# Small VectorE steps placed singly between the products and scans of a selective-state kernel

## The chip, the cores and the metric

One core of one Trainium2 chip runs the whole program. The metric is the device time of one execution in microseconds (us), inputs in HBM to outputs in HBM. Engines are named as in the profile: PE is TensorE, DVE is VectorE, ACT is ScalarE, POOL is GpSimd, SP is SyncE, which here only issues DMAs.

## What is computed

One block over eight batch elements of 512 tokens by 128 channels, all float32. `silu(c) @ wmod` gives scale, shift and gate for each element. Then comes a Mamba-like layer with 256 inner channels, kept as two halves of 128 (`Q = 2`), and 16 states for each channel (`NS = 16`). Then a mixture of experts with a shared expert.

```python
h = layernorm(x) * (1 + ca) + sa
xz = h @ in_proj_w.T                      # x part: causal conv of 4 taps, silu -> u; z part: gate
dt, B, C = split(u @ x_proj_w.T)
delta = softplus(dt @ dt_w.T + dt_b)
state = state * exp(delta * A) + (delta * u) * B      # scan over 512 tokens, per channel and state
y = (sum_n state * C + u * D) * silu(z)
x = x + ga * (y @ out_proj_w.T)
h = layernorm(x) * (1 + cb) + sb
p = softmax(h @ router_w + router_b)      # the two largest of 8 are kept, ties by index
x = x + gb * (shared_expert(h) + sum_e p_e * expert_e(h))   # gelu experts, 128 -> 256 -> 128
```

## The kernel before

**Stages.** The work on the eight elements is pipelined by hand. `pipeline` calls each engine's `slots(b, a, n, m)` eight times: in one slot element `b` is scanned, `a = b - 1` goes through its output projection, second norm, router, experts and residual, `n = b + 1` through convolution, projections and softplus, and `m = b + 2` is loaded and normalised. A slot is called a period here. Each engine runs its instructions strictly in the order in which its own `slots` lists them; only semaphores tie the engines to each other. So the order of the lines is the schedule.

**The scan.** An element has 16 units of 2 states by 512 tokens. For each, ACT makes the decays (`decays`, L885), DVE the product `bc * du` into one PSUM tile (`scan_input`, L1197) and the scan itself (`scan`, L1206), POOL multiplies the state with C (`readout`, L433), and PE adds that into the two Y banks with 8 transposing matmuls (`y_add`, L516). Product `u+1` waits for scan `u` because they share the PSUM tile; scan `u` waits for `yacc_done` of unit `u-4` (a ring of four states); POOL's product `u` waits for DVE's product `u+1` too ("paced"). I call the place after a product and before its scan a P-S gap, and the place after a scan and before the next product an S-P gap. There are 16 of each in a period.

**Element `a` in the same slot.** When unit 15 of `a` is added (`y_add(a, 15)`), DVE multiplies with the gate (`gate_y`, L1216). Then `g_transpose`, `out_proj`, `att_transpose` on PE with `g_rows` and `att_rows` on ACT; `residual` (L1226) with the statistics of the second norm (L1230, L1235) on DVE; `make_rstd` (L420, L423) on POOL; `x1hat` (L1244) on DVE; `x1_transpose` (L616) on PE; `h2_rows` (L992, L995) on ACT; `router` on PE; `split_h2` (L1310) and `logits` (L1254 to L1260) on DVE; `router_e`, a table load and 18 `gelu` (L1014) on ACT beside 18 `up` blocks of three matmuls on PE (L645 to L647), which share three banks; `top2` (L1268 to L1294) on DVE makes the weights `w9`; `weights_transpose` (L654) and `weights_out` (L1007) turn them; then `shared_down` (L662), eight `down` blocks and eight `mix_scaled` / `mix_add`, `acc_rows` (L987), `acc_transpose` (L696) and on DVE `finish` (L1315). Between these PE carries the `y_add`s of `b`. `keep_busy` (L611) issues transposes whose result nobody reads.

**Elements `n` and `m`.** `make_delta` on DVE (L1170 to L1179) ends softplus in four steps after ACT's exponential and logarithm (L957); `delta_x` (L1186) makes `delta * u`. ACT's `skip_term(n)` (L916) and the decays of `n` wait for `delta_done`. `stats` and `xhat` (L1147 to L1158) normalise `m`.

Of the kernel before, what the change touches and what calls it, by code (L numbers as in the profile page):

```python
# [60 lines left out]
def adaln_mamba_moe_kernel(nc, x, in_proj_w, conv_w, conv_b, x_proj_w, dt_w, dt_b, a_log, d_skip,  # L61
# [5 lines left out]
    with ExitStack() as ctx:  # L67
# [25 lines left out]
        before = sb("before", [P, E, E], mybir.dt.bfloat16)  # L93
# [21 lines left out]
        bn = sb("bn", [P, NT, 6])  # L115
        mean_var = sb("mean_var", [P, 2, NT, 2])
# [188 lines left out]
        def _(sp):  # L305
# [47 lines left out]

            def slots(b, a, n, m):
                first_batch = n and isinstance(n.i, int) and n.i == 0
                if m and first_batch:
                    sp.wait_ge(xT_done, m.i)
                    load_x(m)
                if n:
# [3 lines left out]
                if m and n and not first_batch:  # L363

                    load_x(m)
# [3 lines left out]
                if n:  # L369
                    load_bc(n, 0)  # L370
# [3 lines left out]
                if a:  # L374
                    sp.wait_ge(out_done, a.i + 1)
                    sp.dma_start(out[a.i].rearrange("(t p) d -> p t d", p=P),
                                 out_sb[:, :, :]).then_inc(out_stored, 16)
                if b and not is_last(b):

                    load_residual(b)  # L380
                if n:
                    load_bc(n, 1)
                if b and b.i == 1:
# [7 lines left out]
            def tail(a):  # L391
                for t in range(NT):
# [9 lines left out]
        def _(pool):  # L402
            pool.memset(ident[:, :], 0.0).then_inc(const_made, 1)
            pool.memset(before[:, :, :], 1.0).then_inc(const_made, 1)
# [9 lines left out]
            pool.affine_select(out=before[:, :, :], in_=before[:, :, :], pattern=[[1, E], [-1, E]],  # L414
                               compare_op=ALU.is_gt, fill=0.0, base=0,
# [40 lines left out]
        def _(pe):  # L456
# [243 lines left out]
            def slots(b, a, n, m):  # L700
# [44 lines left out]
                if a:  # L745
                    keep_busy(a, n, 5 if b else 12)
# [710 lines left out]
```

## Time and profile before

| | |
|---|---|
| median of 3 runs | 685.6 us (685.33 to 688.16) |
| the profiled execution | 684.8 us, its span 683.1 us |
| DVE busy | 598.3 us, 88% of the span, 713 instructions |
| PE busy | 593.3 us, 87%; weight loads 466.5 us |
| ACT, POOL busy | 489.7 us, 72%; 320.2 us, 47% |
| DVE scans L1206 | 292.2 us in 128, 2283 ns each |
| DVE products L1197 | 157.6 us in 128, 1231 ns each |
| POOL products L433 | 300.1 us in 127, 2363 ns each |
| PE read-out sums L516 | 139.0 us in 1024 matmuls |
| mean DMA rate | 114 GB/s |

Busy shares of two engines near 90% say only that both are candidates. What one waits for, and in which stage, is in the waits and in the timeline. PE's busy time counts pipelined matmuls with a modelled end, so the distance between the starts of two groups is the better measure of what PE needs.

### The profile page before, as it was taken

What the parts mean: (1) busy time and instruction counts of PE and PEld (TensorE: products, weight loads), DVE (VectorE), ACT (ScalarE), POOL (GpSimd) and SP (SyncE); (2) the same over time, 40 slices, a digit from 0 to 9 for tenths busy, and PEclk for the clock granted to TensorE, in tenths of its full rate; (3) what the DMA queues carried; (4) which work ended last, traced back from release to release, by engine and by line L of the source; (5) the groups of instructions that cost most, each with busy time, mean ns of one, the idle gap of its engine ahead of it and who ended that gap; (6) DMA issues with size and microseconds to landing.
All of it is one profiled execution on the core that took longest, in us unless ns stands there. A gap on an engine that the chain in (4) does not pass through costs nothing.

```text
span 683.1 us, 9767 instructions
## 1 busy us (share of the span) xinstructions
PE 593.3 (87%) x3646; PEld 466.5 (68%) x3646; DVE 598.3 (88%) x713; ACT 489.7 (72%) x861; POOL 320.2 (47%) x171
## 2 busy tenths in 40 slices
PE   5684478899989998999989998999979947998897
PEld 4243345689657965788567966787668936798686
DVE  5399999999999999999999999999998999798416
ACT  3689535999589976989589957998598925962460
POOL 1036556446654556446653656446543664464000
PEclk9787589999999999999999999999999968999999
DMA  7423333314432235133531343223522442220000
GB/s 221 161 92 140 123 139 142 125 70 169 163 128 82 108 128 184 62 124 124 173 124 63 124 160 138 83 103 124 179 103 70 176 156 83 103 78 16 1 1 16
DMA packets 26705, 77.87 MB, mean 114 GB/s; under 512 B 3025, under 2 KB 17570, under 8 KB 18466
## 3 DMA queue, kind: packets, MB, share of 16 engines
q1 hardware_dynamic: 26178, 76.82, 31.1%
q8 instruction: 29, 0.48, 0.3%
q10 hardware_dynamic: 480, 0.43, 0.2%
q14 instruction: 18, 0.15, 0.1%
HBM read 74.61 MB, written 2.62 MB: 113 GB/s over the span
## 4 chain that ended last, share of the span: by engine, by line
PE 53%; DVE 31%; issue 7%; ACT 5%; POOL 2%; DMA 1%; DVEq 0%; POOLq 0%; ACTq 0%
DVE state L1206 15%; PE psum L677 12%; PE psum L516 10%; DVE psum L1197 8%; PE psum L543 5%; PE psum L645 5%; PE psum L647 4%; PE psum L646 4%; PE psum L687 3%; POOL state L433 2%; PE psum L662 2%; PE psum L565 1%; ACT L866 1%; DVE out_sb L1244 1%; PE psum L799 1%
## 5 line engine op out<-in xcount | busy, mean ns | idle before, releaser
L433 POOL TENSOR_TENSOR state<-state,bc 128x1024 f32<-128x1024 f32 x127 | 300.1, 2363 | 291.8 <-DVE psum L1197 291.8
L1206 DVE TENSOR_TENSOR_SCAN state<-decay,psum 128x1024 f32<-128x1024 f32 x128 | 292.2, 2283 | 21.9 <-PE psum L516 9.5
L885 ACT ACTIVATE decay<-delta,a_neg 128x511 f32<-128x511 f32 x256 | 166.1, 729 | 10.4 <-DVE state L1206 10.3
L516 PE MATMUL psum<-ident,state 128*128 128x128 f32 x1024 | 139.0, 283 | 33.6 <-POOL state L433 33.4
L1197 DVE TENSOR_TENSOR psum<-bc,du 128x1024 f32<-128x1024 f32 x128 | 157.6, 1231 | 4.8 <-DVE state L1206 0.5
L516 PEld LDWEIGHTS psum<-ident,state 128*128 128x128 f32 x1024 | 120.3, 146 | 56.0 <-POOL state L433 44.9
L677 PE MATMUL psum<-down_w,h 128*128 128x128 f32 x896 | 109.9, 276 | 0.0
L677 PEld LDWEIGHTS psum<-down_w,h 128*128 128x128 f32 x896 | 104.4, 192 | 5.3 <-issue 5.3
L1014 ACT ACTIVATE h<-psum,vec 128x512 f32<-128x512 f32 x144 | 97.0, 688 | 2.1 <-PE psum L647 0.6
L980 ACT ACTIVATE gT_mix<-psum,w 128x128 f32<-128x128 f32 x224 | 64.8, 388 | 20.0 <-PE psum L687 14.4
L645 PE MATMUL psum<-h_hi,up_hi 128*128 128x512 f32 x144 | 59.2, 411 | 10.7 <-DVE h_lo L1310 6.7
L543 PE MATMUL psum<-h_sb,conv_in_wT 128*128 128x512 f32 x128 | 59.9, 614 | 8.8 <-ACT h_sb L895 8.8
L647 PE MATMUL psum<-h_hi,up_lo 128*128 128x512 f32 x144 | 57.7, 401 | 0.0
L646 PE MATMUL psum<-h_lo,up_hi 128*128 128x512 f32 x144 | 57.6, 400 | 0.0
L543 PEld LDWEIGHTS psum<-h_sb,conv_in_wT 128*128 128x128 f32 x128 | 24.3, 199 | 34.6 <-issue 25.4
L645 PEld LDWEIGHTS psum<-h_hi,up_hi 128*128 128x128 f32 x144 | 27.5, 191 | 20.5 <-DVE h_lo L1310 7.3
L687 PE MATMUL psum<-ident,gT_mix 128*128 128x128 f32 x224 | 33.9, 274 | 0.0
L647 PEld LDWEIGHTS psum<-h_hi,up_lo 128*128 128x128 f32 x144 | 27.4, 190 | 6.7
L646 PEld LDWEIGHTS psum<-h_lo,up_hi 128*128 128x128 f32 x144 | 27.6, 191 | 6.0
L687 PEld LDWEIGHTS psum<-ident,gT_mix 128*128 128x128 f32 x224 | 26.0, 141 | 1.5 <-ACT gT_mix L980 1.5
L611 PE MATMUL psum<-ident 128*128 128x128 f32 x210 | 26.2, 273 | 0.0
L906 ACT ACTIVATE du<-psum,vec 128x512 f32<-128x512 f32 x16 | 10.8, 687 | 21.2 <-PE psum L543 18.7
(151 smaller groups left out, 638.3 us busy)
## 6 DMA issues: line engine op xcount, KB each, us to landing
bc<-bc_rows SPq DMA_DIRECT2D x64, 1024.0 KB, 4.7
x_sb<-_attn_hidden_states_dram SPq DMA_DIRECT2D x9, 256.0 KB, 2.8
x<-_attn_hidden_states_dram SPq DMA_DIRECT2D x7, 256.0 KB, 3.0
out_dram<-out_sb SPq DMA_DIRECT2D x7, 256.0 KB, 2.4
h<-in_L_ffn_rw_dram SPq DMA_DIRECT2D x1, 1024.0 KB
bc_rows<-rows SPq DMA_DIRECT2D x8, 64.0 KB, 4.8
h<-in_L_wmod_dram ACTq DMA_DIRECT2D x1, 384.0 KB
h<-in_L_attn_in_proj_w_dram SPq DMA_DIRECT2D x1, 256.0 KB, 4.7
```

The source lines that it names most:

```text
L433: pool.tensor_tensor(state[:, u % STATE_RING, :, :], state[:, u % STATE_RING, :, :], bc[:, pair % BC_RING, 1, first:first + NU, :], ALU.mu ...
L516: last = nc.tensor.matmul(Y[q][:, t * P:(t + 1) * P], state[:, u % STATE_RING, s, t * P:(t + 1) * P], ident[:, :], start=False, stop=(u in ...
L543: last = nc.tensor.matmul(A[q], conv_in_wT[:, q, k, :], h_sb[:, k:k + L], start=(k == 0), stop=(k == KC - 1))
L645: nc.tensor.matmul(bank, high, h2_hi[:, :], start=True, stop=False)
L646: nc.tensor.matmul(bank, high, h2_lo[:, :], start=False, stop=False)
L647: nc.tensor.matmul(bank, low, h2_hi[:, :], start=False, stop=True).then_inc(up_done, 1)
L677: last = nc.tensor.matmul(A[j % 2][:, e * DM:(e + 1) * DM], h1[:, (group * EG + e) * HQ + q, ts], down_w[:, group * EG + e, q, :], start=( ...
L687: last = nc.tensor.matmul(OUTP[:, t * P:(t + 1) * P], mix[:, j % 2, e, :], ident[:, :], start=False, stop=(j == DOWNS - 1 and e == EG - 1) ...
L885: last = nc.scalar.activation(decay[:, r, s, 1:L], delta[:, b.p, q, 1:L], ACT.Exp, scale=a_neg[:, q, k:k + 1])
L1014: nc.scalar.activation(h1[:, m, :], UP_RING[m % 3], ACT.Gelu, bias=vec[:, bias:bias + 1]).then_inc(gelu_done, 1)
L1197: nc.vector.tensor_tensor(IN, bc[:, pair % BC_RING, 0, first:first + NU, :], du[:, b.p, q:q + 1, :].broadcast_to([P, NU, L]), ALU.mult).th ...
L1206: nc.vector.tensor_tensor_scan(state[:, u % STATE_RING, :, :].rearrange("p n t -> p (n t)"), decay[:, u % DECAY_RING, :, :].rearrange("p n ...
```

## The change

- **DVE.** `stats`, `xhat`, `make_delta` and `top2` are cut into single steps. `scan_slots` writes out all gaps of a period by hand and puts one or a few steps into each of 15 P-S gaps and 8 S-P gaps, where before 4 and 6 held any. `residual` and the statistics of the second norm (`stats2`) move from the P-S gap of unit 3 to the S-P gap after scan 2, `x1hat` from after scan 3 to the P-S gap of unit 3, `split_h2` to after scan 3, `logits` to the P-S gap of unit 4. `finish(a - 1)` moves from the end of a period into the next one.
- **Ties.** A table of `1 - 2^-24` and 1 (`tie_scale`) replaces the mask `before`; the comparison needs a scaling and one comparison instead of two comparisons, a product and a sum: two DVE steps fewer for each element.
- **Element `m`.** Its statistics are taken one period earlier (`late`), into a tile of their own (`bn_in`), aggregated in the P-S gap of unit 0, and `xhat` follows in four places up to unit 5.
- **POOL.** `make_rstd` for `m` comes right after product 15 of `a`. `make_rstd` for `a` comes ahead of product 2, and product 2 also waits for `x1hat` to be done.
- **PE.** The three `y_add`s 2, 3 and 4 come after `up` 2, 8 and 14, instead of ahead of the router, after all `up`s, and after `weights_transpose`. `keep_busy` has 24 and 10 transposes instead of 14 and 5. `x_transpose` comes ahead of `down` 2.
- **SP.** The output of `a - 1` is stored at the head of the next slot, then the residual of `a` is loaded; the load of `x` waits for `x_transpose` and lies behind pair 3 of B and C.

```diff
@@ SP slots
-                if m and n and not first_batch:
-                    load_x(m)
+                if a and a.i > 0:
+                    store(Batch(a.i - 1, 1 - a.p))
+                if a:
+                    load_residual(a)
...
+                if b and m and m.i + 1 < B:
+                    sp.wait_ge(xT_done, m.i + 1)
+                    load_x(Batch(m.i + 1, 1 - m.p))
@@ POOL slots
+                if m and (a or not b):
+                    make_rstd(0, stats_done, rstd_eps, rstd_done, m)
                 for u in range(UN - 1):
+                    if a and u == 2:
+                        make_rstd(1, stats2_done, rstd2_eps, rstd2_done, a)
+                        pool.wait_ge(xhat2_done, a.i + 1)
                     if b:
                         readout(b, u)
-                    if a and u == 2:
-                        make_rstd(1, stats2_done, rstd2_eps, rstd2_done, a)
-                    if m and u == 5:
+                    if m and b and not a and u == 1:
                         make_rstd(0, stats_done, rstd_eps, rstd_done, m)
@@ PE slots
-                    keep_busy(a, n, 14)
+                    keep_busy(a, n, 24)
                     x1_transpose(a)
-                if b:
-                    y_add(b, 2)
-                if a:
-                    keep_busy(a, n, 5 if b else 12)
+                    keep_busy(a, n, 10)
                     router(a)
-                    for k in range(M_UP):
+                for k in range(M_UP):
+                    if a:
                         up(a, n, k)
-                if b:
-                    y_add(b, 3)
+                    if b and k in (2, 8, 14):
+                        y_add(b, 2 + (k - 2) // 6)
                 if a:
                     weights_transpose(a)
-                if b:
-                    y_add(b, 4)
                 if a:
                     shared_down(a)
@@ DVE, top2
-                nc.vector.tensor_tensor(gt_eq[:, 1, :, :, :], other, mine, ALU.is_equal
-                nc.vector.tensor_tensor(gt_eq[:, 0, :, :, :], other, mine, ALU.is_gt
...
+                nc.vector.tensor_tensor(
+                    gt_eq[:, 1, :, :, :], pr[:, :, :].unsqueeze(3).broadcast_to([P, NT, E, E]),
+                    tie_scale[:, :, :].unsqueeze(1).broadcast_to([P, NT, E, E]),
+                    ALU.mult).then_inc(prob_step, 1)
...
+                nc.vector.tensor_tensor(
+                    gt_eq[:, 0, :, :, :], pr[:, :, :].unsqueeze(2).broadcast_to([P, NT, E, E]),
+                    gt_eq[:, 1, :, :, :], ALU.is_gt).then_inc(prob_step, 1)
```

The new order of DVE in a period, with I for `scan_input` and S for `scan`: I0 aggr_x, S0 finish(a-1), I1 gate_y, S1 xhat 0 and 1, I2 xhat 2, S2 residual and stats2, I3 x1hat, S3 split_h2, I4 logits, S4, I5 xhat 3, S5 prob_sum, relu_plus_exp and prob_inverse, I6 probs, S6 tie_bars and beaten, I7 ranks, S7 weights, I8, S8 rounded_exp, I9 minus_rounded, S9, I10 plus_log 0, S10, I11 plus_log 1, S11, I12 bn_x 0, S12, I13 bn_x 1, S13, I14 delta_x, S14, I15 bn_x 2 and 3, S15.

## Rows read from the trace of the kernel before

**Rows 1.** The page, chain that ended last: share of the span by engine.

```profile
PE 53%; DVE 31%; issue 7%; ACT 5%; POOL 2%; DMA 1%; DVEq 0%; POOLq 0%; ACTq 0%
```

**Rows 2.** Stretches: length; busy us of PE, PEld, DVE, ACT, POOL; PE's clock; DMA.

```profile
34.00:110.00 76.00, 47.71 (x195) 30.19 (x196) 72.65 (x60) 48.93 (x73) 38.78 (x19) 0.75 0.34 128
334.96:409.97 75.01, 70.70 (x448) 55.67 (x447) 71.49 (x82) 61.65 (x111) 40.15 (x20) 1.00 0.35 125
```

**Rows 3.** DVE timeline, period 4: start us, length us, line, out<-in, idle before.

```profile
333.81 1.23 DVE L1197 TENSOR_TENSOR psum<-bc,du 128x1024 f32<-128x1024 f32 x1
334.96 1.22 DVE L1216 TENSOR_TENSOR gT_mix<-psum,z_silu 128x1024 f32<-128x1024 f32 x1
336.11 2.28 DVE L1206 TENSOR_TENSOR_SCAN state<-decay,psum 128x1024 f32<-128x1024 f32 x1
338.42 1.23 DVE L1197 TENSOR_TENSOR psum<-bc,du 128x1024 f32<-128x1024 f32 x1
339.78 2.29 DVE L1206 TENSOR_TENSOR_SCAN state<-decay,psum 128x1024 f32<-128x1024 f32 x1
...
343.25 0.69 DVE L1226 TENSOR_TENSOR x<-psum,x 128x512 f32<-128x512 f32 x1
...
345.18 2.25 DVE L1206 TENSOR_TENSOR_SCAN state<-decay,psum 128x1024 f32<-128x1024 f32 x1
347.35 1.09 DVE L1244 TENSOR_SCALAR out_sb<-x,mean_var,rstd 128x128 f32<-128x128 f32 x4
```

**Rows 4.** PE timeline, period 4.

```profile
333.83 1.09 PE L516 MATMUL psum<-ident,state 128*128 128x128 f32 x8
...
345.05 1.69 PE L611 MATMUL psum<-ident 128*128 128x128 f32 x14
348.49 0.66 PE L616 MATMUL psum<-ident,out_sb 128*128 128x128 f32 x4 [1.75 <-DVE out_sb L1244]
...
355.54 0.50 PE L645 MATMUL psum<-h_hi,up_hi 128*128 128x512 f32 x1 [0.53 <-ACT h L1014]
...
368.40 1.96 PE L662 MATMUL psum<-h,down_w 128*128 128x512 f32 x4
...
373.22 1.04 PE L516 MATMUL psum<-ident,state 128*128 128x128 f32 x8
```

**Rows 5.** POOL timeline, just ahead of period 4's `gate_y`: product 15 of `a`.

```profile
331.44 2.34 POOL L433 TENSOR_TENSOR state<-state,bc 128x1024 f32<-128x1024 f32 x1 [1.80 <-DVE psum L1197]
```

**Rows 6.** DVE timeline, the same period, `delta_x` in an S-P gap.

```profile
390.11 2.29 DVE L1206 TENSOR_TENSOR_SCAN state<-decay,psum 128x1024 f32<-128x1024 f32 x1
392.31 1.20 DVE L1186 TENSOR_TENSOR du<-du,delta 128x1024 f32<-128x1024 f32 x1
393.43 1.23 DVE L1197 TENSOR_TENSOR psum<-bc,du 128x1024 f32<-128x1024 f32 x1
```

**Rows 7.** DVE by line and shape: busy us, mean ns; one removed step.

```profile
L1283 DVE TENSOR_TENSOR gT_mix<-gT_mix,before 128x256 f32<-128x256 f32 x8 | 3.4, 425 | 0.3
```

**Rows 8.** DVE timeline, end phase: `x1hat` with no scan ahead of it.

```profile
640.07 1.11 DVE L1244 TENSOR_SCALAR out_sb<-x_sb,mean_var,rstd 128x128 f32<-128x128 f32 x4 [1.40 <-POOL rstd L423]
```

**Rows 9.** ACT timeline, period 4.

```profile
350.53 2.55 ACT L885 ACTIVATE decay<-delta,a_neg 128x511 f32<-128x511 f32 x4
...
367.67 0.58 ACT L1007 ACTIVATE rows<-psum 9x512 f32<-9x512 f32 x1 [0.62 <-PE psum L654]
...
381.48 1.34 ACT L916 ACTIVATE skip<-du,vec 128x512 f32<-128x512 f32 x2
...
394.29 1.14 ACT L980 ACTIVATE gT_mix<-psum,w 128x128 f32<-128x128 f32 x4 [0.57 <-PE psum L687]
```

**Rows 10.** DVE timeline, period 6: `gate_y`, scan 7 with its wait, scan 9.

```profile
484.99 1.23 DVE L1216 TENSOR_TENSOR gT_mix<-psum,z_silu 128x1024 f32<-128x1024 f32 x1
...
517.52 2.29 DVE L1206 TENSOR_TENSOR_SCAN state<-decay,psum 128x1024 f32<-128x1024 f32 x1 [2.85 <-PE psum L516]
...
529.20 2.29 DVE L1206 TENSOR_TENSOR_SCAN state<-decay,psum 128x1024 f32<-128x1024 f32 x1
```

More of the change, by code:

```diff
@@ L1319, in slots @@
                 if b:
-                    scan_input(b, 0)
-                    scan(b, 0)
-                    scan_input(b, 1)
+                    scan_slots(b, a, n, m)
+                    return
+                if m:
+                    for t in range(NT):
+                        bn_x(m, t)
+                    nc.vector.memset(pace, 0.0)
+                    aggr_x(m)
+                    for t in range(NT):
+                        xhat(m, t)
+                if n:
+                    split_up_weights()
+                    relu_plus_exp(n)
+                    rounded_exp(n)
+                    minus_rounded(n)
+                    for q in range(Q):
+                        plus_log(n, q)
+                    delta_x(n)
@@ new lines, in scan_slots @@
+            def scan_slots(b, a, n, m):
+                late = Batch(m.i + 1, 1 - m.p) if m and m.i + 1 < B else None
+                new = m if b.i == 0 else None
+                old = m if b.i > 0 else None
+                scan_input(b, 0)
+                if new:
+                    bn_x(new, 0)
+                    bn_x(new, 1)
+                if old:
+                    aggr_x(old)
+                scan(b, 0)
+                if a and a.i > 0:
+                    finish(Batch(a.i - 1, 1 - a.p))
+                scan_input(b, 1)
+                if new:
+                    bn_x(new, 2)
+                    bn_x(new, 3)
@@ L1363, in slots @@
-                for u in range(8, UN):
-                    if b:
-                        scan_input(b, u)
-                    if a:
-                        if u == UN - 1:
-                            finish(a)
-                    if b:
-                        scan(b, u)
-                    if n and u == 12:
-                        delta_x(n)
+                scan(b, 4)
+                if new:
+                    xhat(new, 0)
+                    xhat(new, 1)
+                    xhat(new, 2)
@@ new lines, in scan_slots @@
+                scan_input(b, 11)
+                if n:
+                    plus_log(n, 1)
+                scan(b, 11)
+                scan_input(b, 12)
+                if late:
+                    bn_x(late, 0)
+                scan(b, 12)
+                scan_input(b, 13)
+                if late:
+                    bn_x(late, 1)
+                scan(b, 13)
+                scan_input(b, 14)
+                if n:
+                    delta_x(n)
+                scan(b, 14)
+                scan_input(b, 15)
@@ L1374, in last_readout @@
+                if late:
+                    bn_x(late, 2)
+                    bn_x(late, 3)
+                scan(b, 15)
             def last_readout(b):
```

204 lines of the change are left out of this document (118 added, 86 removed).

## The prediction

> **What bounds the kernel now.** The page shows DVE and PE busy for nearly the same share, so I read the chain of work that ended last first: PE holds 53% of it and DVE 31% [rows 1]. Neither engine sets the pace alone. The stretches say why: in a middle period of 75.01 us DVE is busy for 71.49 and PE for 70.70, at full clock [rows 2]. There are 8 periods. Period 0 has no element `a`: PE is busy for 47.71 of 76 us there, at a mean clock of 0.75, and DVE for 72.65 [rows 2]. Period 0 is DVE's, the middle ones belong to a loop through both.
>
> I measure that loop from the start of `gate_y`, called G; in one middle period G is 334.96 [rows 3] and the next G 409.97 [rows 2]. DVE works on from G almost without idle time. PE's loop is: gate, transposes and projection, `x1hat`, router, `up`, `down`, convolution, y_add 15, gate. POOL's product 15 ends at 331.44 + 2.34 = 333.78 and y_add 15 starts at 333.83 [rows 4, 5]: PE waited for it. The matmuls ahead of it would have let it start some 0.3 us earlier (an estimate: a y_add that waited takes 1.09, and the ones in a stream start 0.87 apart). So PE's own loop is about 74.7 us, DVE's 75.0. This is what to see: PE is 0.3 us behind being the bound.
>
> **DVE: what the gaps are worth.** A plain unit is product at 338.42, scan at 339.78: 1.36 apart, and from a scan to the next product 2.31 (336.11 to 338.42). With `gate_y` (1.22) in a P-S gap the scan comes 2.30 after the product, so the step costs 0.94 of its 1.22 [rows 3]: the gap holds some 0.3 us in which DVE only waits for its own product. `delta_x` (1.20) in an S-P gap makes 3.32 from scan to product instead of 2.31, so it costs 1.0 [rows 6]: 0.2 saved. Eleven more P-S gaps and two more S-P gaps are filled: 11 x 0.3 + 2 x 0.2 = 3.7 us, less where a step is shorter than the gap (bn_aggr, xhat 2 and 3, bn_x and probs nearly vanish, but save no more than they took). `finish` and the second norm change from P-S to S-P and lose 0.1 each. Two tie steps of 0.425 go [rows 7]: 0.9 with their dependence. I add up gap by gap and get 71.0 us for DVE's period, 4.0 less.
>
> The Trainium skill, page "VectorE: DVE Perf Modes", section "The DRAIN you can't avoid", says that a next op waits until the pipe is empty and that semaphores between chained ops cost nothing, which would leave only the removed steps, some 0.9 us. The rows above differ with it, since a step put into a P-S gap is partly free, and I go by the rows.
>
> **PE's loop, with each new term.** All times are from G.
>
> *To x1hat.* The chain gate to `att_transpose` is unchanged; its product, `residual`, starts at 8.29 now [rows 3], but is ready earlier: I put the end of `att_transpose` at 7.3 (an estimate: y_adds 0 and 1, some 1.8 us, end at 10.1 [rows 4], and one `dt_proj` of about 0.9 lies between). In the new order scan 1 is at 1.15, xhat 0 and 1 at 3.36, product 2 at 3.87, xhat 2 at 5.02, scan 2 at 5.27 and `residual` at 7.48, so it doesn't wait. With its statistics it takes 1.93 (343.25 to 345.18). Product 3 is at 9.41. `x1hat` comes 1.40 after the last statistic where nothing covers POOL's work [rows 8]: 10.9. It ends at 12.0, against 13.48 now (347.35 + 1.09).
>
> *A cost that no row shows.* POOL's add and power, most of the 1.40 [rows 8], will run beside product 3, which reads two SBUF tensors; in the old order they lie beside a scan. No row shows the two together. Cost from 0 to 1.07, the rest of product 3 that POOL would have to wait for (below 0 is excluded: POOL was idle anyway). It reaches PE with at most 0.46, because PE itself arrives late: y_add 0 and 1 end at 10.09 (345.05), 24 fillers take 24/13 of what 13 pitches of the 14 took, 2.6 us [rows 4], so `x1_transpose` can start only at 12.7. I take the middle, 0.23.
>
> The Trainium skill, page "SBUF — State Buffer", section "Who interferes with whom", says that a GpSimd instruction and a VectorE one with two SBUF inputs exclude each other for the whole instruction. By it the upper end holds. No row bears it out or speaks against it.
>
> *Router and up.* `x1_transpose` is at 12.7 instead of 13.53, so `split_h2`, ready at 14.9, makes DVE wait 0.75. `up` 3 waits for the first gelu, and that for `router_e` behind four decays (2.55 [rows 9]): 355.54 is 20.58 now [rows 4], then 19.8. y_add 2 lies in that wait, free, as it was ahead of the router. Gain 0.8.
>
> *To shared_down.* From `up` 3 to `shared_down` PE takes 12.86 (355.54 to 368.40) with y_adds 3 and 4 and `weights_transpose` in it. The same matmuls now end in `up` 17 at 32.1. `weights_transpose` waits for w9, which DVE reaches after scan 7, at 32.6: 0.5 lost. Then `weights_out` (0.58 [rows 9]) and its hand-overs have no cover, since y_add 4 has moved: 0.8 lost. `shared_down` starts at 33.95 (34.2 with the 0.23), now at 33.44. Loss 0.5 to 0.75.
>
> *Softplus.* delta is finished by plus_log 1 in the gap of unit 11. Scan 9 has to wait for y_add 5, which starts 4.8 after `shared_down` and takes 1.04 [rows 4]: 39.9. Two units and two such steps further delta is done, at 48.1. ACT reaches `skip_term` at 46.52 now (381.48 [rows 9]) and at about 47.1 then: it waits 1.0, which with its later start makes it 1.1 to 1.3 further behind PE. Its slack against PE is the 0.57 ahead of the last mix step [rows 9]. So 0.4 to 0.7 of PE's loop; I take 0.5. If that slack were not there, it would be 1.1.
>
> *x_transpose, fillers, SP, POOL.* `x_transpose` is the same work earlier. The 5 extra fillers after it lie in the wait for ACT's h2. If that wait were gone they would cost 0.5. On SP the store and the residual load are queued ahead of the rows of `n`, and the load of x behind pair 3 of B and C; `finish` runs well before G, so x1 has over 7 us to land, and B and C of pair 2 are requested only after product 3, so they lose nothing. If a load were late, `residual` or bn_x would wait for it, and DVE has 4 us of slack. On POOL product 2 and all behind it wait for `x1hat`. It starts at 12.1; y_add 2 wants it at 18, so nobody waits.
>
> PE's loop: 74.7 + 0.75 + 0.5 = 75.9, against 75.0 now. DVE's 71.0 is idle time at `gate_y`. Periods 1 to 5: 5 x 0.9 = **+4.5**.
>
> **The other periods.** Period 0 is DVE's. It has no steps of `a`; of those left, seven longer ones or pairs lie in P-S gaps against one before: 6 x 0.3 = 1.8, and xhat 3 and the four bn_aggr nearly vanish, 0.4: -2.2. POOL's `make_rstd` comes beside product 1 of the next period, and product 3 of this one; by the same unknown 0 to 1.2, taken as 0.6: **-1.6**. In period 6 scan 7 waits 2.85 for y_add 3 behind all `up`s [rows 10], and nothing of PE is late afterwards, as there is no convolution behind it. That wait goes; what is late next is y_add 5 at scan 9. Scan 9 is 44.21 after that period's G (529.20 - 484.99) [rows 10] and will be at 40.1; the rest is DVE's and 0.4 dearer: **-3.7**. In period 7, where PE has no work of `n` either, I let the same wait move to scan 9 nearly whole: **-0.3**, an estimate between 0 and -0.7. The end phase holds the same chain; two tie steps less lie beside `up`: 0.
>
> Sum: 684.8 - 1.6 + 4.5 - 3.7 - 0.3 = 683.7 for the profiled execution. The median of the runs is 0.8 above it: **684.5**.
>
> **Rivals.**
> - *DVE keeps the pace.* If the hand-overs (w9, weights_out, skip_term) are covered and the transposes gain more than 0.8, PE's loop falls below 75. At the end DVE's 71.0 decides: 5 x -4 - 6 = 658. Half way, a loop of 73.5: 685.6 - 7.5 - 6 = 672. For it: each loss is under 1 us and three must all be there. Against: PE's work from `shared_down` on (40 us to y_add 15) is the same and none of it waits for DVE.
> - *ACT and PE lose more* (slower). From the point at which ACT is more than 0.57 behind, each further us late in delta reaches every middle period whole. Steps of DVE with two SBUF inputs (minus_rounded, plus_log, delta_x) now start beside POOL's products; if each costs 0.4, and the 1.07 is whole, the loop is 77.3: 5 x 2.3 - 4 = +7.5, 693.
> - *POOL first.* If POOL's product got going ahead of the step in the gap, and they exclude each other, each of six steps would wait about 2.3 us: 14 us a period, less 5 of slack, over 730. Against: a step starts 1.15 after the product's start (334.96 - 333.81) [rows 3], before the product's 1.23 are over, and POOL's product is released only by that end.
> - *The gaps are no cheaper.* The change then doesn't do what it says: DVE's period is 74.1, the loop stays PE's, period 0 gives 0.5 and period 6 3: 686.5.
>
> **Chances.** Forecast 0.50 (its own range 680 to 689), DVE keeps the pace 0.23, ACT and PE lose more 0.19, POOL first 0.03, gaps no cheaper 0.05. The range, 672 to 694, leaves out the far halves of the outer cases. A measurement of this kernel tells about 0.5% (3.4 us) from no change. Faster by more: most of the second case and a quarter of the first, 0.34; slower by more: 0.22; within: 0.44.
>
> **What would show it.** Right: DVE's idle time goes from some 1 us in a middle period to 4 or 5, nearly all at `gate_y` waiting for y_add 15; G to G 75.5 to 76.3; y_add 15 no longer waits for POOL; `weights_transpose` waits for w9 and `shared_down` for `weights_out`; ACT waits for delta at `skip_term`; scan 7 of period 6 doesn't wait, scan 9 does; products of POOL up to 2.36 + 1.2 long where a two-input step shares the gap, if they exclude each other, and `rstd` 1 us later. Wrong: G to G under 74.7, with DVE without idle time; or DVE steps in P-S gaps with starts far above 1.15 after their product.

## The result, and the profile after

The kernel before took 685.47 us (median of 4 runs), the changed one 706.14 us (704.89 to 709.51): a ratio of 1.030, 95% interval 1.027 to 1.034. It is slower by 20.7 us, where the prediction had 684.5 in a range of 672 to 694. The profiled execution took 709.51 us with a span of 707.7, the slowest of the four.

From the starts of `gate_y` (G) in each trace come the lengths of the periods, the measure by which all kernels of this document are compared. P2 is the period that begins with the second G; "to G1" is what lies ahead of the first.

| us | to G1 | P1 | P2 | P3 | P4 | P5 | P6 | P7 |
|---|---|---|---|---|---|---|---|---|
| before | 109.7 | 75.03 | 75.03 | 75.19 | 75.01 | 75.02 | 75.90 | 68.74 |
| changed | 110.2 | 78.14 | 81.73 | 78.17 | 79.12 | 78.17 | 73.98 | 73.34 |

P1, P3 and P5 are 3.0 to 3.2 us longer, and P2 (6.7), P4 (4.1) and P7 (4.6) lose more. P6 gains 1.9. The first view is that of stretches: length, busy us of PE, PEld, DVE, ACT and POOL, PE's granted clock. It answers to [rows 2].

```profile
348.19:427.31 79.12, 73.77 (x463) 58.12 (x462) 71.32 (x77) 61.56 (x111) 43.65 (x20) 0.98 0.34 118
505.48:579.46 73.98, 64.78 (x438) 53.63 (x436) 69.89 (x65) 57.58 (x105) 40.24 (x18) 0.99 0.29 105
```

DVE is busy for 71.32 us of P4 in spite of two tie steps less, against 71.49 before. Something on DVE became longer. The chain of work that ended last has moved too, to ACT above all ([rows 1] had 5%):

```profile
PE 38%; DVE 33%; ACT 12%; issue 8%; DMA 5%; POOL 3%; SPq 0%; DVEq 0%; POOLq 0%; ACTq 0%
```

The waits name the hand-over (engine, line, what it waited for: total us, times, the longest):

```profile
DVE gT_mix L1228 <- PE psum L525: 21.4, 7, 4.0
...
ACT gT_mix L1006 <- DVE gT_mix L1275: 16.1, 8, 2.0
PE psum L654 <- ACT h L1019: 16.0, 6, 2.7
```

Line 1275 is the third step of `logits`. DVE's timeline in P4 (G = 348.19), and under it POOL's, show it:

```profile
360.93 2.28 DVE L1218 TENSOR_TENSOR_SCAN state<-decay,psum 128x1024 f32<-128x1024 f32 x1
363.24 0.76 DVE L1329 TENSOR_TENSOR h_lo<-h,h_hi 128x512 fp32r<-128x512 f32 x1
363.92 1.22 DVE L1209 TENSOR_TENSOR psum<-bc,du 128x1024 f32<-128x1024 f32 x1
365.06 0.18 DVE L1269 TENSOR_TENSOR gT_mix<-psum,router_bias 128x32 f32<-128x32 f32 x1
365.27 0.19 DVE L1273 TENSOR_REDUCE router_stats<-gT_mix 128x4 f32<-128x32 f32 x1
365.49 2.17 DVE L1275 TENSOR_TENSOR gT_mix<-gT_mix,router_stats 128x32 f32<-128x32 f32 x1
367.58 2.27 DVE L1218 TENSOR_TENSOR_SCAN state<-decay,psum 128x1024 f32<-128x1024 f32 x1
```

```profile
357.69 1.09 POOL L426 TENSOR_TENSOR rstd<-mean_var,constants 128x4 f32<-128x4 f32 x1 [2.00 <-DVE mean_var L1250]
358.85 1.01 POOL L429 TENSOR_TENSOR rstd<-rstd,constants 128x4 f32<-128x4 f32 x1
361.09 2.37 POOL L439 TENSOR_TENSOR state<-state,bc 128x1024 f32<-128x1024 f32 x1 [1.23 <-DVE out_sb L1259]
365.22 2.39 POOL L439 TENSOR_TENSOR state<-state,bc 128x1024 f32<-128x1024 f32 x1 [1.77 <-DVE psum L1209]
```

A step on 128x32 elements takes 2.17 us: it ends at 367.66, right behind POOL's product 3 (365.22 + 2.39 = 367.61). The step of the same size ahead of it, a reduction, takes 0.19 with that product beside it. In the changed kernel all seven `logits` that lie beside a product of POOL have such a third step (2.02 to 2.17), and the eighth, in the end phase with POOL idle, takes 0.19. In the kernel before, where `logits` stood behind a scan, it took 0.19 every time. Likewise POOL's add ahead of `rstd` takes 1.09 beside product 3 of DVE, and 0.20 elsewhere.

What that does to PE, in PE's timeline of P4, to be laid beside [rows 4]:

```profile
370.07 0.79 PE L654 MATMUL psum<-h_hi,up_hi 128*128 128x512 f32 x1 [2.68 <-ACT h L1019]
370.66 0.63 PE L655 MATMUL psum<-h_lo,up_hi 128*128 128x512 f32 x1
371.08 0.63 PE L656 MATMUL psum<-h_hi,up_lo 128*128 128x512 f32 x1
...
383.71 0.60 PE L663 MATMUL psum<-ident,w 128*9 128x128 f32 x4
385.35 1.95 PE L671 MATMUL psum<-h,down_w 128*128 128x512 f32 x4 [1.04 <-ACT rows L1012]
```

`up` 3 starts at G + 21.88, after PE stood for 2.68 us; before it was G + 20.58 with 0.53. In this period the first matmuls behind the wait start 0.43 us apart instead of 0.235, until 372.79: the granted clock is 0.50 in that stretch, the lower of its two levels (1.2 of 2.4 GHz). `shared_down` starts at G + 37.16 here and at G + 36.2 in the periods without that, against 33.44.

P2 has a cause of its own, on SP's queue (start us, issue time) and then on DVE:

```profile
182.72 0.43 SPq L389 DMA_DIRECT2D gate_row<-gateT  x1
192.92 0.32 SPq L391 DMA_DIRECT2D gate_row_sb<-gate_row  x1
193.29 0.43 SPq L357 DMA_DIRECT2D out_dram<-out_sb  x1
193.76 0.51 SPq L352 DMA_DIRECT2D x<-_attn_hidden_states_dram  x1
```

```profile
199.27 0.69 DVE L1238 TENSOR_TENSOR x<-psum,x 128x512 f32<-128x512 f32 x1 [3.49 <-DMA x<-_attn_hidden_states_dram]
```

`gate_row`'s round trip through DRAM, done once, holds SP for 10.2 us (182.72 to 192.92). The store and the residual's load now stand behind it, so `residual` waits 3.49 us.

### The profile page after: what moved, and what is told of

It is laid out like the page before. It is cut to its first block, busy times and chain, and to the rows that moved or that the text cites. A ratio compares the mean times of both kernels' runs of the same rounds, so it can differ in the third digit from the quotient of the medians.

```text
span 707.7 us, 9968 instructions
## 1 busy us (share of the span) xinstructions
PE 616.1 (87%) x3751; PEld 483.4 (68%) x3751; DVE 597.2 (84%) x691; ACT 488.1 (69%) x861; POOL 346.5 (49%) x171
## 4 chain that ended last, share of the span: by engine, by line
PE 38%; DVE 33%; ACT 12%; issue 8%; DMA 5%; POOL 3%; SPq 0%; DVEq 0%; POOLq 0%; ACTq 0%
DVE state L1218 17%; DVE psum L1209 9%; PE psum L525 6%; PE psum L552 5%; ACT gT_mix L985 3%; ACT decay L890 3%; PE psum L686 3%; PE psum L620 2%; POOL state L439 2%; PE psum L602 2%; PE psum L671 2%; PE psum L654 2%; PE psum L655 2%; PE psum L656 2%; DMA x_sb<-_attn_hidden_states_dram 2%
## 5 line engine op out<-in xcount | busy, mean ns | idle before, releaser
L439 POOL TENSOR_TENSOR state<-state,bc 128x1024 f32<-128x1024 f32 x127 | 318.2, 2505 | 270.1 <-DVE psum L1209 261.5
L654 PE MATMUL psum<-h_hi,up_hi 128*128 128x512 f32 x144 | 62.7, 435 | 17.4 <-ACT h L1019 16.0
L552 PE MATMUL psum<-h_sb,conv_in_wT 128*128 128x512 f32 x128 | 61.8, 630 | 9.2 <-ACT h_sb L900 9.2
L655 PE MATMUL psum<-h_lo,up_hi 128*128 128x512 f32 x144 | 59.9, 416 | 0.0
L656 PE MATMUL psum<-h_hi,up_lo 128*128 128x512 f32 x144 | 59.4, 412 | 0.0
L654 PEld LDWEIGHTS psum<-h_hi,up_hi 128*128 128x128 f32 x144 | 29.0, 201 | 25.1 <-ACT h L1019 17.8
L620 PE MATMUL psum<-ident 128*128 128x128 f32 x315 | 38.3, 275 | 0.0
L620 PEld LDWEIGHTS psum<-ident 128*128 128x128 f32 x315 | 35.5, 142 | 0.5 <-issue 0.5
L426 POOL TENSOR_TENSOR rstd<-mean_var,constants 128x4 f32<-128x4 f32 x16 | 9.4, 588 | 44.6 <-DVE mean_var L1250 31.3
```

The costliest lines, as they stand in the source:

```text
L439: pool.tensor_tensor(state[:, u % STATE_RING, :, :], state[:, u % STATE_RING, :, :], bc[:, pair % BC_RING, 1, first:first + NU, :], ALU.mu ...
L552: last = nc.tensor.matmul(A[q], conv_in_wT[:, q, k, :], h_sb[:, k:k + L], start=(k == 0), stop=(k == KC - 1))
L620: nc.tensor.transpose(A[1][:, 0:P], ident[:, :], ident[:, :])
L654: nc.tensor.matmul(bank, high, h2_hi[:, :], start=True, stop=False)
L655: nc.tensor.matmul(bank, high, h2_lo[:, :], start=False, stop=False)
L656: nc.tensor.matmul(bank, low, h2_hi[:, :], start=False, stop=True).then_inc(up_done, 1)
```

## The experiments

Each kernel was timed beside the one before on the same chip; the ratio is to that. The first table gives the periods of all of them, and the texts behind it what each is. They are told in the order of the argument; e1 to e4 ran first, then c1, e5, e6 and e8, then d1, c1f and c2, and d2 to d4 last.

| kernel | median us | ratio (95%) | P1 | P2 | P3 | P4 | P5 | P6 | P7 |
|---|---|---|---|---|---|---|---|---|---|
| e1 | 692.08 | 1.007 (1.003 to 1.010) | 76.55 | 79.07 | 76.29 | 76.26 | 77.63 | 71.77 | 69.11 |
| e2 | 704.26 | 1.025 (1.020 to 1.031) | 78.15 | 78.16 | 79.17 | 78.15 | 78.18 | 75.15 | 70.17 |
| e3 | 707.94 | 1.030 (1.024 to 1.036) | 78.15 | 80.66 | 79.48 | 78.18 | 79.74 | 74.46 | 72.16 |
| e4 | 721.25 | 1.050 (1.045 to 1.055) | 80.78 | 79.68 | 80.96 | 79.66 | 80.66 | 80.51 | 72.29 |
| e6 | 696.62 | 1.017 (1.011 to 1.023) | 78.07 | 76.14 | 77.96 | 78.05 | 76.16 | 77.02 | 69.43 |
| e8 | 710.07 | 1.036 (1.031 to 1.041) | 79.31 | 79.26 | 78.34 | 78.17 | 79.24 | 79.04 | 71.49 |
| e5 | 726.30 | 1.057 (1.051 to 1.064) | 81.14 | 84.35 | 81.80 | 81.35 | 80.12 | 77.17 | 74.50 |
| d1 | 691.77 | 1.008 (1.005 to 1.010) | 76.68 | 79.33 | 76.40 | 76.38 | 77.76 | 72.05 | 67.82 |
| d2 | 688.03 | 1.002 (0.998 to 1.006) | 74.54 | 82.47 | 74.57 | 74.56 | 74.57 | 72.69 | 68.41 |
| d3 | 682.78 | 0.995 (0.992 to 0.997) | 74.54 | 74.58 | 74.58 | 74.58 | 75.96 | 72.66 | 68.51 |
| d4 | 703.41 | 1.024 (1.019 to 1.029) | 78.06 | 76.55 | 77.91 | 78.07 | 78.07 | 74.58 | 72.29 |
| c1 | 680.55 | 0.990 (0.987 to 0.994) | 75.39 | 75.37 | 75.36 | 75.33 | 75.32 | 72.15 | 66.99 |
| c1f | 681.34 | 0.992 (0.988 to 0.995) | 75.36 | 75.03 | 75.02 | 75.02 | 75.02 | 72.13 | 67.72 |
| c2 | 675.98 | 0.984 (0.980 to 0.988) | 73.88 | 74.74 | 74.74 | 73.88 | 73.91 | 72.71 | 68.00 |

### Is it POOL's product that holds the step?

**e1**, in the changed kernel's POOL slots:

```
 if b and a and u == 3:
     pool.wait_ge(lg_step, 3 * a.i + 3)      # added: product 3 waits for logits
 if b:
     readout(b, u)
```

> The changed kernel with one wait more: POOL's product 3 waits until the three steps of logits are done. Theory A (exclusion): the third step of logits, with two SBUF inputs, was held for 2.17 us by POOL's product 3. Here it takes 0.19, up 3 starts some 2 us earlier (G + 19.9 instead of G + 21.9), POOL's product starts about 1 us later and nobody waits for it; middle periods of 76.2 instead of 78.2 us, and with period 7 the whole is 14 to 18 us shorter, 688 to 692 us. Theory B (the hand-overs of w9 and weights_out, the fillers and the late delta carry the loss): the third step is beside the path, and the time changes by less than 3 us, 703 to 708.

DVE's and PE's timelines in P4 (G = 343.17):

```profile
360.25 0.19 DVE L1275 TENSOR_REDUCE router_stats<-gT_mix 128x4 f32<-128x32 f32 x1
360.47 0.19 DVE L1277 TENSOR_TENSOR gT_mix<-gT_mix,router_stats 128x32 f32<-128x32 f32 x1
```

```profile
363.07 0.50 PE L656 MATMUL psum<-h_hi,up_hi 128*128 128x512 f32 x1 [0.71 <-ACT h L1021]
363.41 0.39 PE L657 MATMUL psum<-h_lo,up_hi 128*128 128x512 f32 x1
```

The step takes 0.19, `up` 3 starts at G + 19.90, the `up`s run at full clock, P4 is 76.26 and the median, 692.1, is at the upper end of what was expected: Theory A. One added wait on POOL, an engine with time to spare, gives back 14 of the 20.7 us. P2 and P5 of e1 stay longer, P2 by the wait for a load that is shown above, and P5 by 1.4 us because `y_add` 0 and 1 ran slowly, as in d3 below.

**e4** makes the one step from the other side, in the kernel before:

```
-                    logits(a)                # behind split_h2, ahead of product 5
 scan_input(b, 5)
+if a: logits(a)
 scan(b, 5)
```

> The kernel before with one part of the change alone: logits moved from behind split_h2 (ahead of product 5) to behind product 5 (ahead of scan 5). Theory A (exclusion): POOL's product 4 is released by the end of product 5 and holds the third step of logits for about 2.1 us instead of 0.19; logits ends 3.5 us later, up 3 starts some 3.5 us later, of which PE's loop has 0.3 to spare: periods 3.0 to 3.6 longer, times 6 or 7, 18 to 25 us: 704 to 710. Theory B (no exclusion, a step in a product-scan gap is partly free): the third step takes 0.19, logits ends 1.5 us later, periods 1.2 longer: +7 to +8.5 us, 693 to 694, with DVE 0.3 us a period better off.

**e6** is e4 with POOL's product 4 waiting for `logits`:

> The same as e4 (the kernel before with logits in the gap of product 5), but POOL's product 4 waits for logits. Theory A (exclusion): the third step takes 0.19, logits ends 1.15 later than before the change, up 3 at G + 21.7 instead of 23.7, periods of 75.9 to 76.5 instead of 79.7 to 80.7; 692 to 697 against 721 for e4. Theory B (the place in the gap itself, or DVE's waits, made e4 slow): no less than 710.

e4's third step takes 2.20 us and `up` 3 starts at G + 23.71; with POOL held back (e6) it takes 0.19 and `up` 3 starts at G + 21.7. 721 against 697 us: with all that follows from each, the place in the gap costs some 10 us by itself and POOL's product 25 more. e6's median lies in Theory A's 692 to 697, but only P2 and P5 are in its 75.9 to 76.5. In P1, P3 and P4 (78.0) the matmuls from `up` 3 to `up` 17 take 11.6 to 11.9 us instead of 9.93, although PE's wait ahead of them is no longer there than in P2 (0.5 to 1.0 us; P2's is 1.67). In P4 (G = 344.09) the lower clock sets in at the end of `up` 1, in a row of matmuls without a gap and some 1.5 us ahead of that wait:

```profile
363.03 0.50 PE L649 MATMUL psum<-h_hi,up_lo 128*128 128x512 f32 x1
363.33 0.63 PE L647 MATMUL psum<-h_hi,up_hi 128*128 128x512 f32 x1
363.76 0.63 PE L648 MATMUL psum<-h_lo,up_hi 128*128 128x512 f32 x1
```

So the wait ahead of `up` 3 isn't the only thing that takes the clock down. e4 itself was over its expected 704 to 710, and its periods grew by 4.65 to 5.8 us where `up` 3 is only 3.1 later. PE's timeline of e4's P4 shows where the rest is:

```profile
374.68 0.79 PE L645 MATMUL psum<-h_hi,up_hi 128*128 128x512 f32 x1 [3.67 <-ACT h L1014]
375.27 0.63 PE L646 MATMUL psum<-h_lo,up_hi 128*128 128x512 f32 x1
375.70 0.63 PE L647 MATMUL psum<-h_hi,up_lo 128*128 128x512 f32 x1
```

### What a wait of PE costs besides itself

**e8** is e4 with filler transposes in PE's wait:

```
 for k in range(M_UP):
+    if k == 3:
+        pe.wait_ge(lg_step, 3 * a.i + 1)
+        for _ in range(32):
+            nc.tensor.transpose(MISC[:, 0:P], ident[:, :], ident[:, :])
     up(a, n, k)
```

> The same as e4, with 32 filler transposes (0.11 us each) on PE between up 2 and up 3, where PE is idle for 3.67 us and the following up matmuls start 0.43 instead of 0.235 apart. Theory A (the idle time lets the clock fall, and that adds to the wait): up 3 starts at G + 23.7 as in e4, all matmuls behind it are 0.235 apart, from up 3 to up 17 it takes 9.95 instead of 11.5 to 12.6, the mean granted clock rises from 0.92, periods are 1.5 to 2.5 shorter, 705 to 711 us. Theory B (the slow matmuls come from something else, a port or PSUM): no change, 719 to 723.

```profile
368.19 3.66 PE L752 MATMUL psum<-ident 128*128 128x128 f32 x32
372.04 0.50 PE L645 MATMUL psum<-h_hi,up_hi 128*128 128x512 f32 x1 [0.19 <-ACT h L1018]
372.37 0.40 PE L646 MATMUL psum<-h_lo,up_hi 128*128 128x512 f32 x1
372.61 0.40 PE L647 MATMUL psum<-h_hi,up_lo 128*128 128x512 f32 x1
```

This is Theory A: the same start of `up` 3 in P4 (G + 23.72), and from there to `up` 17 it takes 9.94 us instead of 11.4 to 12.6. 721.3 becomes 710.1: a third of what e4 costs is the lower clock behind the wait. In three periods the fillers themselves ran at the lower clock and made `up` 3 1.1 us late (G + 24.8), so a filler isn't free either.

### The other wait that the change added

**e5** is the changed kernel without `pool.wait_ge(xhat2_done, a.i + 1)` ahead of product 2.

> The changed kernel without POOL's wait for x1hat ahead of its product 2. x1hat is four steps with one SBUF tensor and two scalars per partition each. Theory A (exclusion reaches these steps too): POOL's product 2 starts with rstd and holds x1hat for some 2.3 us, x1_transpose is 2.3 later, periods at least 2 us longer, 718 to 725. Theory B (only steps with two SBUF tensors are held): x1hat takes 1.1 as now, the time stays within 3 us of the changed kernel's, 703 to 709.

POOL's and DVE's timelines in P4:

```profile
369.10 2.37 POOL L439 TENSOR_TENSOR state<-state,bc 128x1024 f32<-128x1024 f32 x1
```

```profile
369.17 3.15 DVE L1258 TENSOR_SCALAR out_sb<-x,mean_var,rstd 128x128 f32<-128x128 f32 x4 [1.16 <-POOL rstd L429]
```

`x1hat`, one SBUF tensor and two scalars a step, is held too: 3.15 us for 1.11. The time rises by 20 us, to 726.3, which is 1.3 above Theory A's 718 to 725 and far from Theory B. The wait that the prediction passed over as costless is what keeps the changed kernel from that time.

### The rest of the loss

**e2** moves `gate_row`'s round trip on SP ahead of `load_bc(n, 0)` in the same slot:

> The changed kernel with the round trip of gate_row on SP moved ahead of the loads of B and C of n in the same slot, so that it no longer stands ahead of the store and the load of the residual. Theory A (SP's order made period 2 3.5 us longer than its neighbours): bn-free DVE at residual in period 2, period 2 of 78.2 instead of 81.7 us, the whole 3 to 3.6 us shorter, about 702.7. Theory B (the load of period 2 was late for another reason, the queue's traffic): period 2 stays at 81 to 82, no change.

P2 is 78.16 like P1 and P4, 3.6 less: Theory A. The median, 704.3, falls by only 1.9 us, within what the medians vary; the period is the clearer measure.

**e3** sets `y_add` 4 behind `weights_transpose` again, `k in (2, 8)` instead of `(2, 8, 14)`:

> The changed kernel with y_add 4 behind weights_transpose again, as before the change, instead of ahead of up 15. Theory A (hand-over without cover): y_add 4 fills PE's wait for weights_out; shared_down 0.8 us earlier, 5 to 7 periods of 0.6 to 0.8 shorter each, 3 to 5.5 us in all, about 702. Theory B (scan 8 then waits for y_add 4, or weights_transpose itself is what is late): less than 1.5 us.

Nothing gained (Theory B): `shared_down` starts at G + 36.2 in an undisturbed period, as in the changed kernel. `up` 17 comes 0.85 earlier and `weights_transpose` doesn't, because w9 leaves DVE at G + 34.6 in both. **d1** therefore takes e1 and e3 together and brings w9 forward:

```
 if a:
     prob_inverse(a)                          # gap between scan 5 and product 6
+    probs(a); tie_bars(a); beaten(a); ranks(a); weights(a)
```

> The changed kernel with e1's wait of POOL and e3's y_add 4 behind weights_transpose, and with the rest of the top 2 (probs, tie_bars, beaten, ranks, weights) in the gap between scan 5 and product 6, where the sum and its inverse are, so that w9 is there some 7 us earlier. To be compared with e1 (692.1 us, shared_down at G + 34.3, middle periods 76.3). Theory A (w9 came 0.65 us late, and behind it weights_out had no cover, which is why e3 alone gave nothing): weights_transpose follows up 17 at once, shared_down at G + 32.8, periods 1.3 to 1.5 us shorter, 683 to 686. Theory B (the loop behind shared_down, delta's above all, sets the pace): shared_down earlier but periods less than 0.5 us shorter, 690 to 692.

`shared_down` starts at G + 33.0, 1.3 earlier than in e1, and P4 is 76.38, no shorter than e1's 76.26. Theory B. ACT's timeline shows who takes the gain:

```profile
388.64 1.34 ACT L925 ACTIVATE skip<-du,vec 128x512 f32<-128x512 f32 x2 [1.97 <-DVE delta L1195]
```

`skip_term` waits 1.97 us for delta and starts at G + 48.61; in the kernel before it is 46.52 [rows 9]. **d2** finishes delta one unit earlier:

```
 scan(b, 8)
 if n: rounded_exp(n)
+      minus_rounded(n)                      # was behind product 9
 scan_input(b, 9)
+if n: plus_log(n, 0)                         # was behind product 10
 ...
 scan_input(b, 10)
+if n: plus_log(n, 1)                         # was behind product 11
```

> d1 with delta finished one unit earlier: minus_rounded behind rounded_exp in the gap between scan 8 and product 9, plus_log 0 behind product 9, plus_log 1 behind product 10 (in d1 plus_log 1 is behind product 11). To be compared with d1 (691.8 us, middle periods 76.4, shared_down at G + 33.0, skip_term at G + 48.6 after 1.97 of waiting for delta) and with the kernel before (periods 75.0, skip_term at 46.5). Theory A (after e1's cure it is delta's lateness that holds the loop; w9's hid it, so neither e3 nor d1 could gain): skip_term doesn't wait and starts at G + 46.5 to 46.8, the middle periods are 74.6 to 75.1, the whole 8 us shorter, 682 to 685. Theory B (delta is beside the path, and the mix chain or the earlier x_transpose holds the loop at 76.4): no change, 690 to 693.

```profile
388.92 1.34 ACT L925 ACTIVATE skip<-du,vec 128x512 f32<-128x512 f32 x2
```

`skip_term` at G + 46.5 without a wait, four middle periods of 74.54 to 74.57: Theory A. No kernel here has delta early without w9 early, so how the 1.8 us a period (76.38 to 74.56) divide between the two isn't measured. But the total, 688.0, is above the expected 682 to 685, and P2 is 82.5 us: `residual` waits 5.44 us for the same load as above, and PE's next `up`s start 0.43 apart as well. **d3** adds e2's move, and **d4** is d3 without POOL's wait for `logits`:

> d2 with e2's place for the round trip of gate_row. With it all four causes found are undone in the changed kernel (POOL's product ahead of the third step of logits, w9 and y_add 4, late delta, gate_row), and DVE's steps otherwise stand in the gaps as the change put them. Theory A (these four are the whole loss): period 2 falls from 82.5 us in d2 to 74.6, all middle periods are 74.5 to 74.7, and the whole is 679 to 681 us, 5 us below the kernel before. Theory B (something else of the new order costs as well, and period 2 of d2 was disturbed by chance): 685 or more.

> d3 without POOL's wait for logits: the only cause of the four that is left in. Theory A: the third step of logits takes 2.17 us again and up 3 starts at G + 21.9 instead of 19.9; nothing else is late now, so all of it reaches the loop: middle periods 76.5 where the clock holds and up to 77.9 where up 3's wait takes it down; 14 to 20 us more than d3, 694 to 700. Theory B (part of it is hidden behind something else): periods under 75.8, less than 9 us.

d3: P2 is 74.58, the whole 682.78, 0.5% under the kernel before. It is some 2 us above what was expected; P5 has 1.4 us more than its neighbours, and there `y_add` 0 and 1 ran at the lower clock (3.41 us for 1.97). So with these four undone the loss is gone, and what is left, 0.5%, is what the rest of the change gains; the four were not each taken out of d3 alone, only the held step was. d4: that step alone costs 20.6 us, a little more than Theory A's 14 to 20. Of its periods P2 is 76.55, where the clock held (2.0 more than d3: the wait itself), and P1, P4 and P5 are 78.06 to 78.07, where it fell behind the wait (3.5 more than d3's undisturbed 74.58). P3 (77.91) lost nearly as much in another place: there `y_add` 0 and 1 were slow.

### A better order

**c1** (made before d1 to d4) puts the steps where the rows of e1 to e4 said: residual, statistics and `x1hat` between scan 2 and product 3, so that `rstd` and `x1hat` lie beside nothing; `split_h2` and `logits` behind scan 3; w9 and delta early; 14 fillers, `y_add` 4 and `gate_row` as above, and no wait of POOL.

> The changed kernel with its parts placed so that no step with two SBUF inputs comes second in a product-scan gap and no wait of PE's loop is made longer. Residual, statistics and x1hat all stand in the gap between scan 2 and product 3 (DVE waits for POOL's rstd there, and POOL's small steps run beside nothing of DVE); split_h2 and logits between scan 3 and product 4; the softmax sums between scan 4 and product 5; tie_bars behind product 5, beaten behind product 6, ranks and weights behind scan 6 (w9 some 7 us earlier); rounded and minus behind scan 8, plus_log behind products 9 and 10; 14 fillers ahead of x1_transpose; y_add 4 behind weights_transpose; gate_row ahead of B and C of n; POOL no longer waits for x1hat. Theory A (exclusion in logits, w9 late, gate_row): logits ends at G + 16.6 instead of 19.5, up 3 at G + 19.0, shared_down at 32 to 32.8, periods of 73.3 to 74.5 us, the whole 670 to 678. Theory B (something else of the new order, such as x_transpose ahead of the downs, holds the loop above 75): periods 75 to 76, 682 to 688.

It takes 680.55 us, 1.0% less than the kernel before, but more than its 670 to 678, with periods of 75.3 to 75.4, in Theory B's 75 to 76. `logits` ends at G + 16.6 as planned, `shared_down` starts at G + 33.8 and not at 32 to 32.8. Two rows show what else was there, DVE's behind product 5 and PE's at the router (G = 334.45):

```profile
356.21 0.42 DVE L1296 TENSOR_TENSOR gT_mix<-gT_mix,tie_scale 128x256 f32<-128x256 f32 x1
356.55 2.42 DVE L1165 TENSOR_SCALAR x_sb<-x_sb,mean_var,rstd 128x128 f32<-128x128 f32 x1
```

```profile
350.59 0.51 PE L653 MATMUL psum<-h_hi,up_hi 128*128 128x512 f32 x1 [0.50 <-DVE h_lo L1330]
350.92 0.60 PE L654 MATMUL psum<-h_lo,up_hi 128*128 128x512 f32 x1
351.32 0.63 PE L655 MATMUL psum<-h_hi,up_lo 128*128 128x512 f32 x1
```

I had made the same mistake again: step 3 of `xhat` stands second behind product 5 and is held (2.42 for 0.34). And with fewer fillers `up` 0 to 2 run at the lower clock, so that `up` 3 starts at G + 20.7 instead of 19.0. **c1f** has 17 fillers for 10 ahead of the router and 4 behind it:

> c1 with 7 fillers more ahead of the router (17 for 10) and 4 between the router and up 0, all in time in which PE is idle (0.84 and 0.50 us). In c1 the matmuls of router and of up 0 to 2 run at half rate (8 in 1.06 us; 0.43 apart) and up 3 starts at G + 20.7. Theory A (the idle time takes the clock down): up 0 to 2 are 0.235 apart, up 3 at G + 19.2 to 19.5, periods 73.9 to 74.5 (DVE, idle for 1.0 us, then sets the pace at 74.3), the whole 5 us shorter, 674 to 677. Theory B (the rate of up 0 to 2 is set by the gelus or by a load): no change, 679 to 682.

**c2** is c1f with that step of `xhat` alone behind product 3:

> c1f and, besides, step 3 of xhat moved from second place behind product 5, where it took 2.42 us instead of 0.34, into the gap behind product 3, alone. Theory A (steps of xhat, one SBUF tensor and two scalars, are held by POOL's product as those with two tensors are): it takes 0.34 there, DVE's own period falls from 74.3 to 72.3 and w9 comes 2 us earlier; with full clock in up 0 to 2 the periods are 73.5 to 74.0, the whole 670 to 675. Theory B (ranks and weights, not POOL, made w9 late, and DVE is not near being the bound): no gain over c1f.

c1f brings `up` 3 to G + 19.24, as its Theory A had it, but hardly any time (681.34, as its Theory B had it): `weights_transpose` now waits 1.23 us for w9, which stands behind the held `xhat` step, and the periods go only from 75.3 to 75.0. In c2 the `xhat` step takes 0.34 and the kernel gains 5.4 us more: 675.98, 1.6% faster than the kernel before and 1 us above its expected 670 to 675. Its middle periods are 73.9 where the clock holds and 74.7 where `y_add` 0 and 1 are slow.

## Why the prediction was wrong

**What bounds the kernel, and DVE's share: right.** DVE's idle time did go to `gate_y` (3.98 us at the end of each of P1 to P5), and DVE's own period comes out nearly as forecast: P1's 78.14 less its waits at `gate_y` (3.98) and scan 9 (0.66) and the 1.96 of the held step leaves 71.5, where 71.0 stood. A step in a P-S gap is cheaper, as the rows said.

The prediction had set against this the Trainium skill, page "VectorE: DVE Perf Modes", section "The DRAIN you can't avoid", read as if only the removed steps (0.9 us) could gain. The same section adds that a next op that is not held starts earlier, which the prediction left out. The trace agrees with that: DVE's period went down by 3.5.

**To x1hat: right, near its upper end.** `residual` G + 7.41 (7.48 forecast), `x1hat` G + 11.70 (10.9, and 0 to 1.07 on top), `x1_transpose` 12.88 (12.7). The 0.8 is POOL's add held by product 3, 1.09 for 0.20. None of this reached PE: the 24 fillers end at G + 12.86, and with the middle that was taken, 0.23, the forecast for `x1_transpose` was 12.93. So this term was no miss. But it was the same exclusion, and I had priced it as half true, and at this one place only.

**Router and up: the step that failed.** The forecast let `up` 3 move 0.8 us earlier, to G + 19.8; it moved 1.3 later, to 21.88. Nearly all of the 2.08 between them is the 1.98 by which `logits`' third step was held (2.17 for 0.19); e1, which takes only that away, has `up` 3 at G + 19.90. Everything behind it was sized right: from `up` 3 to `shared_down` 14.15 forecast and 14.3 measured, w9 0.5 and 0.6 late, from `shared_down` to the next G 41.7 and 42.0. Put 2.08 into the sum's 75.9 and it gives 78.0 (77.8 if `up` 3 is counted from 20.03, with the 0.23 that the 75.9 contains); P1, P3 and P5 are 78.14 to 78.17.

The prediction had this mechanism as the rival "POOL first", with the right price (2.3 us a step), and gave it 0.03. Its argument, that a step starts 1.15 after its product and so ahead of POOL, is true of the first step in a gap alone: the step in [rows 3] was a single one (and, with one input in PSUM, of a kind that no row here shows held). `logits` has three, each waiting for the one ahead, and the third comes 0.43 us after the first; POOL's product started 0.16 after the first. I counted the steps that have two SBUF inputs, and not their places in the gap. The case "ACT and PE lose more" held the other half, small losses of each step, and also ended at 693.

The Trainium skill, page "SBUF — State Buffer", section "Who interferes with whom", says that whichever of the two starts first keeps the other out for its whole instruction, for steps of VectorE with two SBUF inputs and for `tensor_scalar` in a two-port mode, and not for `tensor_reduce` or, outside such a mode, for one SBUF input. The traces agree: 2.17 us (two inputs) and 2.42 (`xhat`, a `tensor_scalar`) against 0.19 for the reduction and 2.28 for the scan, both with POOL's product beside them. Whether `xhat` runs in a two-port mode no row shows by itself. The prediction named the section and then asked it one question too few.

**The clock: left out.** The sum had no term for it. d4 against d3 shows 2.0 us for a 2 us wait where the clock held and 3.5 where it fell; P4 (+1.0 over P3 and P5) and P7, where `up` 3 to `up` 17 took 14.4 us against 11.6 in P1, are of this kind.

**SP: wrong in P2.** "If a load were late" was priced by DVE's slack of 4 us, for each period alike. The load was late once, behind `gate_row`, at `residual`, which lies ahead of PE's loop and not in DVE's slack: 3.6 us (e2). In d2, where P1 is shorter and the load so comes later in P2, it is 7.9 (against d3): 5.5 until `x1hat`, and the rest is the clock.

**Softplus: right, and hidden.** `skip_term` waited 0.56 for the 1.0 forecast, since everything ahead of it was later. As soon as that was undone (d1) it waited 1.97, and held the loop alone.

**The other periods.** P6 was forecast to gain 3.7 and gained 1.9, P7 0.3 and lost 4.6; both carry the held step, P7 the clock as well. With the step free (e1) P6 is 71.8, 4.1 less than before, and P7 69.1. Period 0 was forecast to gain 1.6: from its first product to G1 it takes 70.3 us against 71.5, a gain of 1.2 (0.6 to 1.2 over the kernels e1, e2, d3 and c2). The whole time to G1 doesn't show it, as the setup ahead of it varies by more. The end phase, from the eighth G on, was put at 0 and lost 1.5; its `up` 1 to `up` 3 ran at the lower clock (0.43 us apart). That isn't the new order: from the same place c2 takes 53.4 us, as the kernel before does, and e8, which is built on the kernel before, 54.95.

The sum of the misses in P1 to P5, by the periods: 5 x 2.08 for the held step, 3.6 in P2, 1.0 in P4, together 15.0; measured less forecast is 20.05 - 4.5 = 15.6. The profiled execution was 709.5 us for the forecast 683.7; the other 10.2 of these 25.8 us are 1.8 in P6, 4.9 in P7, 1.5 in the end phase and 2.0 ahead of the first G.

## What to carry to other kernels

Before a small step goes into a gap of a busy engine, ask which other engine the neighbour's end releases, and count the step's place in the gap: the first one starts ahead, the second and third start behind, and if both engines want the same access, 0.2 us becomes the other's whole instruction. Hold the engine with time to spare back by one wait rather than let it race. Losses on a loop hide one another: undoing one of them (e3, d1) showed nothing until the next was undone as well, so test them in a stack and then take out one at a time (d4).

## What the runs showed of the hardware

- A `tensor_scalar` with one SBUF tensor and two per-partition scalars is held by POOL's product like a step with two SBUF tensors: 2.42 us for 0.34, 3.15 for 1.11. Reductions, `bn_aggr`, scans with one operand in PSUM, and `gate_y` (PSUM and SBUF) are not: each was seen to start behind POOL's product and keep its time (0.19, 0.15 for one of the four `bn_aggr`, 2.28 and 1.22).
- It goes both ways: POOL's product takes 3.19 to 3.27 us instead of 2.36 where a 1.22 us step with two SBUF inputs starts first (the changed kernel, `minus_rounded` and the product beside it):

```profile
389.42 1.22 DVE L1186 TENSOR_TENSOR delta<-delta,g_soft 128x1024 f32<-128x1024 f32 x1
389.64 3.21 POOL L439 TENSOR_TENSOR state<-state,bc 128x1024 f32<-128x1024 f32 x1 [3.02 <-DVE psum L1209]
```

- With POOL's small steps, too, it counts who starts first. The add takes 1.09 for 0.20 and the power 1.92 for 1.01 when they begin some 0.17 us behind a product of DVE, as here in period 0 of the changed kernel. Begun 0.5 us ahead of product 1, the power takes its 1.01 and the product its 1.22, though they overlap. So a POOL instruction doesn't exclude DVE for all of its recorded time in every case; for which part it does isn't settled by these runs.

```profile
109.01 1.23 DVE L1209 TENSOR_TENSOR psum<-bc,du 128x1024 f32<-128x1024 f32 x1
109.18 1.92 POOL L429 TENSOR_TENSOR rstd<-rstd,constants 128x4 f32<-128x4 f32 x1
```

- A wait of 2.7 us on PE is followed in some periods by matmuls at half the rate and in others not, in one and the same execution (d4: 78.07 and 76.55). The lower clock also set in without such a wait, in the middle of a row of `up`s (e6, P4) and at `y_add` 0 and 1 (d3, P5). Which it will be wasn't explained by anything tried here.
